# Weight preparation inside the projection's program, and 25 units of row maxima placed in its last six chunks

## The chip, the cores and the metric

One core of one Trainium2 chip runs the whole program. The metric is the device time of one launch in microseconds. Shown are the median of three runs and one profiled execution.

## The reference

For x of 8 batches x 1024 tokens x 256 features, in float32:

```
xn = layernorm(x)
Q, K, V = xn wq^T, xn wk^T, xn wv^T     # 16 heads of 16; RoPE on Q and K
s  = softmax(causal(Q K^T / 4)) V wo^T
g  = silu( (silu(xn wg^T) * (xn wu^T)) wd^T )   # wg, wu, wd: int32 / 127, hidden 768
out = x + s * g
```

The four attention weights are 256 x 256 float32. The three FFN weights are integers from -127 to 127.

## The kernel before

The program has three blocks, one behind the other; at each border all engines meet.

**The preparation block** (lines 216 to 379). SP loads the four attention weights into raw, the first half of batch 0 of x, gate and up integers, the down integers, the second half of x and the sine and cosine table trig (lines 230 to 238). VectorE takes the absolute maximum of all four weights in one instruction (L309), the layer norm's statistics of the first 512 tokens (L168, L175), and builds a power-of-two scale per weight (L314 to L325). TensorE transposes every weight in 128 x 128 pieces through PSUM, 19 banks in all (L378). For the four float weights ScalarE writes the high float16 part (L350) and VectorE the low one (L334). For the integers VectorE casts to float32 (L330), and the two engines take the transposed banks in turn (L301, L355). VectorE normalises the first tokens (L184) after the four weights. GpSimd clears vs, fills ks (L261), and computes the inverse root (L192, L194) and the low part of the tokens (L204). ScalarE writes their high part (L199), and SP issues two DMA transposes (L213), which give xTh and xTl.

**The projection block** (lines 393 to 702) works through 16 chunks of 512 tokens, two per batch. Batches 0 to 6 are a hardware loop, the last batch is written out (`over_batches`). In a chunk TensorE does Q and K (L639, three products of high and low parts), V (L647), the six gate and up products (L662) and the down products of high and low parts (L676). VectorE turns Q and K (L484), multiplies gate by up (L493) and takes low parts; ScalarE takes high parts, SiLU and the copies; GpSimd adds the rotation's terms (L544) and takes low parts (L452, L460). While a chunk runs, the next chunk's tokens are normalised, split and transposed. Results go to HBM. With the last batch SP also loads the stacks of three head groups for the attention of batch 0 (`load_stacks`, L754 to L757; 24 DMAs in one place).

**Units of maxima.** The attention needs each query's largest score before it exponentiates. A group is 4 heads of one batch, 32 groups in all. Its maxima are 18 units: TensorE computes two PSUM banks of scores (L773, causal mask added by L781), and VectorE reduces them (L797, `maximum`). Then `join_max` (L1118) joins the pieces, TensorE transposes the 32 x 128 result (L1340), `negate_max` (L1124) scales and negates it, `split_max` on GpSimd (L1045, L1047) makes two float16 rows, and `load_max` on SP (L986) writes them by 4 DMAs into the query stacks, where they ride along in the score matmul. The projection block holds 17 units of group (0,0) in its last two chunks, at places named after the work they follow (`peek`, PSUM banks 0 and 1):

```
PEEKS = ({"ffn1": 0, "ffn2": 1, "ffn3": 2, "ffn4": 3, "down0": 4, "down2": 5, "down4": 6},
         {"q0": 7, "q1": 8, "k0": 9, "ffn1": 10, "ffn2": 11, "ffn3": 12, "ffn4": 13, "down0": 14, "down2": 15, "down4": 16})
```

**The attention block** begins with `first_maxima`: unit 17 of group (0,0), its join, transpose, negation, split and load, and 7 units of group (0,1). Then come the 32 groups, written out. In a group TensorE follows a hand-written order of 36 turns, 18 E (a score matmul L1316 for ScalarE's exponential L1245) and 18 M (a unit of maxima of a coming group), over three pairs of PSUM banks; a turn waits until the instruction that read its pair three turns before is done (`wait_slot`). Products with V (L1333), output transposes (L1353, L1361) and the output projection (L1369) stand at fixed turns. The first score of a group waits for its maxima rows (mx_ld).

Of the kernel before, what the change touches and what calls it, by code (L numbers as in the profile page):

```python
# [13 lines left out]
P = 128  # L14
# [58 lines left out]
def earlier(step, n):  # L73
    return step[0], step[1] - n
# [14 lines left out]
def project_phase(nc, ps, keep, x, wq, wk, wv, wo, w_gate, w_up, w_down, cs, scratch):  # L89
# [5 lines left out]
    with ctx:  # L95
# [9 lines left out]
        wguT = sb("wguT", [P, 2, KD, HID], F16)  # L105
        wdT = sb("wdT", [P, MH, D], F16)
        trig = sb("trig", [P, 2, 2, S], F32)
        table = sb("table1", [1, 1], F32)
        negh = sb("negh", [P, CT], F32)
# [13 lines left out]
        s_const = sem("s_const")  # L123
        s_ones = sem("s_ones")
        s_one = sem("s_one")
        s_max, s_maxT, s_scale, s_low = sem("s_max"), sem("s_maxT"), sem("s_scale"), sem("s_low")
        s_held = sem("s_held")
        s_unfilled = sem("s_unfilled")
        s_wload = sem("s_wload")
        s_iload = [sem(f"s_iload{i}") for i in range(3)]  # L130
        s_prep = sem("s_prep")
        s_wt = sem("s_wt")
        s_we = [sem(f"s_we{i}") for i in range(2)]
# [82 lines left out]
        with ExitStack() as pre, nc.Block() as block:  # L216
            raw = pre.enter_context(nc.sbuf_tensor("raw", [P, 8, D], F32))
            rawi = pre.enter_context(nc.sbuf_tensor("rawi", [P, 18, D], I32))
            rawf = pre.enter_context(nc.sbuf_tensor("rawf", [P, 18, D], F32))
            wmax = pre.enter_context(nc.sbuf_tensor("wmax", [P, 4], F32))  # L220
            wmaxT = pre.enter_context(nc.sbuf_tensor("wmaxT", [4, 1], F32))
            ones4 = pre.enter_context(nc.sbuf_tensor("ones4", [4, P], F32))
            diag4 = pre.enter_context(nc.sbuf_tensor("diag4", [4, 4], F32))
            wbits = pre.enter_context(nc.sbuf_tensor("wbits", [P, 4], I32))
            wscale = pre.enter_context(nc.sbuf_tensor("wscale", [P, 4], F32))
            SCALE_STEPS = 9

            @block.sync
            def _(sp):
                for i, w in enumerate((wq, wk, wv, wo)):  # L230
                    sp.dma_start(raw[:, 2 * i:2 * i + 2, :], w.rearrange("(m p) d -> p m d", p=P)).then_inc(s_wload, 16)
                sp.dma_start(xs[:, 0], x_v[0, 0]).then_inc(x_ld[0].sem, 16)
                for i, w in enumerate((w_gate, w_up)):
                    sp.dma_start(rawi[:, 6 * i:6 * i + 6, :], w.rearrange("(m p) d -> p m d", p=P)).then_inc(s_iload[i], 16)
                sp.dma_start(rawi[:, 12:18, :].rearrange("p (a m) e -> p a (m e)", a=2),
                             w_down.rearrange("(a p) e -> p a e", p=P)).then_inc(s_iload[2], 16)
                sp.dma_start(xs[:, 1], x_v[0, 1]).then_inc(x_ld[1].sem, 16)
                sp.dma_start(trig[:, :, :, :], cs[:, :, :, :]).then_inc(s_const, 16)
                for s in (t_hi, t_lo):
                    s.start(sp)  # L240
                transpose_tokens(sp, (0, 0))

            @block.gpsimd
            def _(pool):
                for s in (ln_ve, ln_rs, x_lo):
                    s.start(pool)
                ch = Chain(pool, s_prep)
                ch(pool.memset(ident[:, :], 0.0))
                ch(pool.affine_select(out=ident[:, :], in_=ident[:, :], compare_op=ALU.not_equal, fill=1.0,
                                      base=0, pattern=[[-1, P]], channel_multiplier=1))  # L250
                ch(pool.memset(ones4[:, :], 1.0))
                ch(pool.memset(identh[:, :], 0.0))
                ch(pool.affine_select(out=identh[:, :], in_=identh[:, :], compare_op=ALU.not_equal, fill=1.0,
                                      base=0, pattern=[[-1, P]], channel_multiplier=1))
                ch(pool.memset(negh[:, :], -0.5))
                ch(pool.memset(table[:, :], 0.0))
                ch(pool.memset(vs[:, :, :, :], 0.0))
                ch(pool.memset(vs[:, :, :, DK:DK + 1], 1.0))

                for g in range(NG):  # L260
                    pool.memset(keep["ks"][g].rearrange("p j s -> p (j s)").bitcast(F32), MAX_UNITS).then_inc(s_ones, 1)  # L261
                inverse_root(pool, (0, 0))
                low_tokens(pool, (0, 0))


            banks = []
            split = []
            for i in range(4):
                srcs = [raw[:, 2 * i + m, kd * P:(kd + 1) * P] for kd in range(KD) for m in range(2)]
                flat = lambda t: t.rearrange("p k e -> p (k e)")  # L270
                banks.append((srcs, []))
                if i < 2:

                    split.append([([wqkT[:, hl, kd, 2 * i + eo, :].rearrange("p (i h) -> p i h", h=H) for hl in range(2)], kd, eo)
                                  for kd in range(KD) for eo in range(2)])
                else:
# [1231 lines left out]
```

## Time and profile before

| what | us |
|---|---|
| median of 3 runs (1251.95 to 1253.29) | 1253.18 |
| the profiled execution | 1253.75 |
| its span, first to last instruction | 1252.0 |
| TensorE busy | 1196.9 |
| VectorE busy | 1009.0 |
| ScalarE busy | 851.2 |
| GpSimd busy | 601.7 |
| mean granted TensorE clock | 0.985 |

The profile's engines are PE (TensorE), PEld (its weight loads), DVE (VectorE), ACT (ScalarE), POOL (GpSimd) and SPq (the DMA issues of SyncE). A bracket at the end of a timeline row gives how long the engine stood idle before it and who released it. Matmul durations overlap the next matmul, so the distance of two starts says what one costs.

### The profile page before, as it was taken

Reading aid. Unit: us, or ns where it says so; the run is one execution under the profiler, and the core shown is the slowest. Engines: PE = TensorE matmul, PEld = TensorE weight load, DVE = VectorE, ACT = ScalarE, POOL = GpSimd, SP = SyncE. Lnnn points to the kernel's source line nnn. Section 1 sums busy time; section 2 is a strip of 40 time slices with the busy share of each in tenths; the row PEclk is TensorE's granted clock in tenths of the full one; section 3 lists DMA queues with packets and bytes.
Section 4 is the critical chain, followed back from the end, with each engine's and each line's share of the span. In section 5 each row is a group of like instructions: output and inputs, shape, how many; then the busy total and the mean of one; then the engine's idle time right before and its main releaser. Section 6 shows DMA issues by size and latency. Waiting matters only on the chain.

```text
span 1252.0 us, 30431 instructions
## 1 busy us (share of the span) xinstructions
PE 1196.9 (96%) x10743; PEld 558.0 (45%) x10743; DVE 1009.0 (81%) x1229; ACT 851.2 (68%) x1074; POOL 601.7 (48%) x934
## 2 busy tenths in 40 slices
PE   4999999999999799999999999999999999999997
PEld 3556656656654333334433443344334433443333
DVE  5666666666668789899999999999999999999943
ACT  3455465465453367678887888788788878887884
POOL 4665665665663222235444544454445345534554
PEclk9999999999999789999999999999999999999999
DMA  7444544544565311223313323243143233331222
GB/s 243 128 145 165 163 145 161 166 146 157 168 155 153 97 44 44 77 59 106 94 44 111 79 86 95 62 119 95 45 116 103 57 95 82 99 95 44 70 70 85
DMA packets 152228, 133.48 MB, mean 107 GB/s; under 512 B 44720, under 2 KB 137392, under 8 KB 151984
## 3 DMA queue, kind: packets, MB, share of 16 engines
q1 hardware_dynamic: 152112, 131.90, 35.7%
q8 instruction: 77, 1.26, 0.4%
q14 instruction: 39, 0.32, 0.1%
HBM read 72.61 MB, written 50.33 MB: 98 GB/s over the span
## 4 chain that ended last, share of the span: by engine, by line
PE 56%; issue 5%; DVE 2%; ACT 1%; DMA 1%; SPq 1%; POOL 0%; DVEq 0%; ACTq 0%; POOLq 0%
PE ps L1333 21%; PE ps L1316 13%; PE ps L773 11%; PE ps L1369 4%; PE ps L781 3%; PE ps L1353 3%; DVE mxp L797 2%; PE ps L1361 2%; ACT pr L1245 1%; DMA qs<-mp 1%; PE ps L1340 1%; SPq L986 1%; ACT ot L1252 0%; DVE yt L1181 0%; POOL ah L1065 0%
## 5 line engine op out<-in xcount | busy, mean ns | idle before, releaser
L797 DVE TENSOR_REDUCE mxp<-ps 128x2 f32<-128x1024 f32 (+2 forms) x576 | 683.6, 1222 | 64.8 <-PE ps L773 37.0
L1245 ACT ACTIVATE pr<-ps 128x1024 f32<-128x1024 f32 x576 | 570.0, 1033 | 172.1 <-PE ps L1316 164.5
L1333 PE MATMUL ps<-pr,vt 128*32 128x512 f32 (+3 forms) x3072 | 316.5, 500 | 1.4 <-ACT ot L1252 0.9
L1055 POOL TENSOR_SCALAR_AFFINE_SELECT pr<-pr 128x256 f32<-128x256 f32 (+1 forms) x448 | 192.1, 449 | 125.8 <-ACT pr L1245 124.6
L1316 PE MATMUL ps<-qs,ks 50*128 50x512 f16 (+3 forms) x1536 | 227.1, 331 | 14.2 <-DMA qs<-mp 3.5
L773 PE MATMUL ps<-ks,qs 48*128 48x512 f16 (+2 forms) x1792 | 228.0, 308 | 9.8 <-DVE mxp L797 5.0
L1045 POOL TENSOR_SCALAR mp<-mneg 32x128 f16<-32x128 f32 x32 | 9.2, 288 | 319.2 <-issue 305.6
L1316 PEld LDWEIGHTS ps<-qs,ks 50*128 50x128 f16 x1536 | 64.8, 94 | 214.2 <-issue 205.9
L662 PE MATMUL ps<-xTh,wguT 128*128 128x512 f16 x384 | 145.9, 380 | 1.5 <-ACT vs L571 1.2
L662 PE MATMUL ps<-xTl,wguT 128*128 128x512 f16 x384 | 145.8, 380 | 0.0
L773 PEld LDWEIGHTS ps<-ks,qs 48*128 48x128 f16 x1792 | 82.1, 94 | 138.1 <-issue 119.2
L493 DVE SCALAR_TENSOR_TENSOR h<-ps,sg 128x512 f32<-128x512 f32 x96 | 66.0, 688 | 59.3 <-ACT sg L579 44.3
L1333 PEld LDWEIGHTS ps<-pr,vt 128*32 128x32 f32 x3072 | 67.7, 109 | 86.2 <-issue 76.3
L566 ACT ACTIVATE parts<-rr 128x1024 f16<-128x1024 f32 x32 | 33.8, 1057 | 79.1 <-POOL rr L544 79.1
L781 PE MATMUL ps<-future,pick 64*128 64x128 bf16 (+3 forms) x1024 | 86.6, 245 | 0.0
L579 ACT ACTIVATE sg<-ps 128x512 f32<-128x512 f32 x96 | 57.1, 595 | 39.9 <-PE ps L662 30.9
L460 POOL TENSOR_TENSOR hl<-h,hh 128x512 f16<-128x512 f32 x64 | 72.8, 1157 | 21.3 <-ACT hh L585 21.2
L639 PE MATMUL ps<-xTh,wqkT 128*128 128x512 f16 x256 | 80.7, 385 | 2.4 <-DMA xTl<-xl 2.4
L544 POOL TENSOR_TENSOR rr<-rot 128x1024 f32<-128x1024 f32 x32 | 74.8, 2363 | 15.2 <-DVE rot L484 15.2
L484 DVE TENSOR_TENSOR rot<-ps,trig 128x1024 f32<-128x1024 f32 x64 | 75.3, 1219 | 8.4 <-PE ps L639 8.4
L585 ACT ACTIVATE hh<-h 128x512 f16<-128x512 f32 x96 | 58.3, 624 | 4.7 <-DVE h L493 4.0
L662 PEld LDWEIGHTS ps<-xTh,wguT 128*128 128x128 f16 x384 | 37.4, 97 | 47.6 <-DVE h L493 3.3
(107 smaller groups left out, 1315.6 us busy)
## 6 DMA issues: line engine op xcount, KB each, us to landing
v_d<-vs SPq DMA_DIRECT2D x16, 1024.0 KB, 4.9
vt<-v_d SPq DMA_DIRECT2D x32, 512.0 KB, 4.1
xs<-in_L_attn_x SPq DMA_DIRECT2D x16, 512.0 KB, 4.2
q_parts_d<-parts SPq DMA_DIRECT2D x16, 512.0 KB, 2.9
k_parts_d<-parts SPq DMA_DIRECT2D x16, 512.0 KB, 2.9
gate_d<-gs SPq DMA_DIRECT2D x16, 512.0 KB, 3.2
qs<-q_parts_d SPq DMA_DIRECT2D x64, 128.0 KB, 3.0
ks<-k_parts_d SPq DMA_DIRECT2D x64, 128.0 KB, 3.1
```

The costliest lines, as they stand in the source:

```text
L460: eng.tensor_tensor(hl[:, m], h32[:, m % NH], hh[:, m], ALU.subtract).then_inc((lo_pool if m < LOW_POOL else lo_dve).sem, 1)
L484: ins = dve.tensor_tensor(tq[i][:, t], ps[:, (Q0, K0)[i]:(Q0, K0)[i] + 2, :], trig[:, t, :, c * CH:(c + 1) * CH], ALU.mult)
L544: pool.tensor_tensor(rr[i][:, :, :], tq[i][:, :, 0, :], tq[i][:, :, 1, :], ALU.add).then_inc(rot_add.sem, 1)
L639: ins = pe.matmul(ps[:, (Q0, K0)[i] + eo, :], wqkT[:, wp, kd, 2 * i + eo, :], xx[:, c, :, kd, :], start=n == 0, stop=n == len(terms) - 1)
L662: ins = pe.matmul(ps[:, FFN[m] + gu, :], wguT[:, gu, kd, m * P:(m + 1) * P], xx[:, c, :, kd, :], start=n == 0, stop=n == 2 * KD - 1)
L773: ins = pe.matmul(ps[:, slot + t, n * w:(n + 1) * w], qs[r, j, qb * P:(qb + 1) * P], ks[r, j, lo:lo + w], start=n == 0, stop=not any(maske ...
L781: ins = pe.matmul(o, pick[r, half ^ t, :], future[r, half ^ t, 0:len(pieces), half * TILE:P], start=False, stop=half == 1, skip_group_chec ...
L797: dve.tensor_reduce(dst, ps[:, slot:slot + 2, :].rearrange("p t (n s) -> p (t n) s", s=w), axis=AX.X, op=ALU.max).then_inc(keep["max_dve"] ...
L1055: pool.affine_select(out=blk, in_=blk, compare_op=ALU.is_ge, fill=0.0, base=0, pattern=[[0, 2], [0, len(hs)], [1, P]], channel_multiplier= ...
L1245: act.activation(probs(step, s).rearrange("p (t j) s -> p t j s", t=2)[:, :, hs[0]:hs[-1] + 1, 0:w], ps[:, slot:slot + 2, 0:w * len(hs)].r ...
L1316: ins = pe.matmul(ps[:, slot + t, o:o + w], ks[g][r, j, kb * P:(kb + 1) * P], qs[g][r, j, lo:lo + w], start=o == 0, stop=True, skip_group_ ...
L1333: ins = pe.matmul(ps[VW * j:VW * (j + 1), O0, lo - c * CH:CH], vt[g % 2][:, kb, j, :], probs(step, s)[:, j, at:at + w], start=first, stop= ...
```

## The change

The preparation block goes. Its work moves into the projection block, ahead of and into the first chunk:

- SP loads x first, then the weights, each with a semaphore of its own. The table trig is loaded in two halves by token half, each in two DMAs, between the other loads.
- VectorE takes one maximum per weight: three before the normalisation of the first tokens, one after. The float weights are still transposed by TensorE and split by ScalarE and VectorE; query and key parts come before the first chunk, V's in its beginning, and wo's low part after the low part of Q.
- The integers are cast by ScalarE to float16 and transposed by three DMA transposes on SP, with no work of TensorE or VectorE. wguT and wdT have another layout for it.
- GpSimd clears vs and builds identh in the first chunk, and the constants of pick and future at its end; before, they stood ahead of the first chunk.
- Before the loop now stands batch 0 written out, then a loop over batches 1 to 4, then batches 5 to 7 written out.
- The 17 units in the last two chunks become 25 in the last six: all 18 of group (0,0) in five chunks, and in the last one 7 of group (0,1). The join's transpose stands at place q0 of the last chunk, then negation, split and load of the maxima in the projection's block. `first_maxima` goes from the attention block, whose first TensorE instruction is now the first score.
- SP loads one head group's stacks per chunk, in three chunks.

```diff
-        with ExitStack() as pre, nc.Block() as block:
...
             def over_batches(eng, chunk):
 
-                with eng.Fori(0, B - 1) as b:
+                for c in range(HALVES):
+                    chunk((0, c), True)
+                with eng.Fori(1, B - WRITTEN_OUT) as b:
                     for c in range(HALVES):
                         chunk((b, c), True)
-                for c in range(HALVES):
-                    chunk((B - 1, c), c + 1 < HALVES)
+                for b in range(B - WRITTEN_OUT, B):
+                    for c in range(HALVES):
+                        chunk((b, c), (b, c) != (B - 1, HALVES - 1))
 
             @block.sync
             def _(sp):
...
+                sp.dma_start(xs[:, 0], x_v[0, 0]).then_inc(x_ld[0].sem, 16)
+                for i, w in enumerate((wq, wk, wv, wo)):
+                    sp.dma_start(raw[:, 2 * i:2 * i + 2, :], w.rearrange("(m p) d -> p m d", p=P)).then_inc(s_wload[i], 16)
+                sp.dma_start(xs[:, 1], x_v[0, 1]).then_inc(x_ld[1].sem, 16)
+                for i, w in enumerate((w_gate, w_up)):
+                    sp.dma_start(rawi[:, MH * i:MH * (i + 1), :], w.rearrange("(m p) d -> p m d", p=P)).then_inc(s_iload[i], 16)
...
+                def transpose_ints(i):
+                    sp.wait_ge(s_cast, i + 1)
+                    dst = wguT[:, i].rearrange("p m k t -> p (m k) t") if i < 2 else wdT.rearrange("p k m t -> p (k m) t")
+                    sp.dma_start_transpose(dst[:, :, :], rawh[:, MH * i:MH * (i + 1), :].rearrange("p m d -> p (m d)")).then_inc(s_ints[i], 16)
+
+                transpose_tokens(sp, (0, 0))
+                load_trig(0)
+                sp.dma_start(rawi[:, 2 * MH:3 * MH, :].rearrange("p (a m) e -> p a (m e)", a=2),
+                             w_down.rearrange("(a p) e -> p a e", p=P)).then_inc(s_iload[2], 16)
+                transpose_ints(0)
+                transpose_ints(1)
+                load_trig(1)
+                transpose_ints(2)
...
                 over_batches(sp, chunk)
+                load_max(sp, keep, (0, 0))
...
+                stats(dve, (0, 0))
+                for i in range(3):
+                    weight_max(i)
+                normalise(dve, (0, 0))
+                weight_max(3)
...
+                stats(dve, (0, 1))
+                weight_low(0)
+                weight_low(1)
...
+                high_tokens(act, (0, 0))
+                act.wait_ge(s_wt, 4)
+                act.wait_ge(s_scale, SCALED)
+                weight_high(0)
+                weight_high(1)
+                weight_high(2)
+                cast_ints(0)
+                cast_ints(1)
...
                 def peek(step, place):
-                    if isinstance(step[0], int) and place in PEEKS[step[1]]:
...
+                    if joined(step) and place == "q0":
+                        transpose_max(pe, ps, keep, (0, 0), T0)
+                    if peeked(step, place):
+                        ms, u = peeked(step, place)
+                        if ms == (0, 1) and u == 0:
+                            pe.wait_ge(keep["mx_neg"].sem, keep["mx_neg"].after((0, 0)))
...
+WRITTEN_OUT = 3
+SHIFT = 7
+PLACES = (((3, 0), ("down0", "down2")), ((3, 1), ("ffn1", "ffn3", "down0", "down2")), ((2, 0), ("ffn1", "ffn3", "down0", "down2")),
+          ((2, 1), ("ffn1", "ffn3", "down0", "down2")), ((1, 0), ("ffn1", "ffn3", "down0", "down2")),
+          ((1, 1), ("q1", "k0", "ffn1", "ffn2", "ffn3", "ffn4", "down0")))
+PEEKED = [((0, 0), u) for u in range(18)] + [((0, 1), u) for u in range(SHIFT)]
...
-                for n, (ms, u) in enumerate(first_maxima):
-                    if n == 0:
-                        pe.wait_ge(max_dve.sem, max_dve.after((0, 0), PEEKED))
-                    if n >= SLOTS:
-                        pe.wait_ge(max_dve.sem, max_dve.after(first_maxima[n - SLOTS][0], first_maxima[n - SLOTS][1] + 1))
-                    queries_by_keys(pe, ps, keep, s_held, ms, u, slot_of(n - len(first_maxima)))
-                    if (ms, u) == ((0, 0), NM - 1):
-                        transpose_max((0, 0))
```

## Rows read from the trace of the kernel before

**Rows 1.** The page's part 1: busy time, share, instructions.

```profile
PE 1196.9 (96%) x10743; PEld 558.0 (45%) x10743; DVE 1009.0 (81%) x1229; ACT 851.2 (68%) x1074; POOL 601.7 (48%) x934
```

**Rows 2.** Windows by stage: length; busy us of each engine; clock; DMA share, GB/s.

```profile
0.00:28.31 28.31, 10.70 (x56) 9.32 (x56) 16.65 (x45) 9.17 (x21) 11.71 (x22) 0.94 0.73 250
...
56.68:337.48 280.80, 280.80 (x1730) 168.88 (x1728) 184.92 (x301) 150.29 (x228) 175.38 (x120) 1.00 0.49 157
...
359.65:387.02 27.37, 26.87 (x176) 14.71 (x174) 20.38 (x23) 12.68 (x21) 14.41 (x9) 1.00 0.89 202
387.02:417.24 30.22, 28.79 (x192) 15.07 (x190) 24.68 (x23) 10.81 (x18) 11.37 (x7) 1.00 0.24 88
...
429.64:458.64 29.00, 25.98 (x207) 8.56 (x208) 23.43 (x24) 17.90 (x19) 6.03 (x15) 0.73 0.08 17
458.64:484.33 25.69, 23.17 (x242) 8.64 (x243) 23.77 (x25) 19.12 (x21) 6.97 (x17) 1.00 0.20 56
```

**Rows 3.** Timeline of the start: start us, us, engine, line, instruction, tiles.

```profile
3.09 1.80 POOL L257 MEMSET vs<- 128x2048 f32 x1
4.50 2.53 SPq L235 DMA_DIRECT2D rawi<-in_L_ffn_w_down  x1
5.22 3.62 POOL L261 MEMSET ks<- 128x1024 f32 x4
6.98 2.29 DVE L309 TENSOR_REDUCE wmax<-raw 128x4 f32<-128x2048 f32 x1 [6.98 <-DMA raw<-in_L_attn_wo]
...
11.70 1.03 POOL L194 TENSOR_TENSOR rstd<-ve,negh 128x4 f32<-128x4 f32 x1
...
13.69 2.17 ACT L350 ACTIVATE wqkT<-ps,wscale 128x128 f16<-128x128 f32 x8 [10.42 <-DVE oscale L325]
14.87 1.12 DVE L334 SCALAR_TENSOR_TENSOR wqkT<-ps,wscale,wqkT 128x128 f16<-128x128 f32 x4 [0.21 <-ACT wqkT L350]
...
20.00 1.37 DVE L184 TENSOR_SCALAR xn<-xs,mv,rstd 128x256 f32<-128x256 f32 x4
...
28.31 0.39 PE L639 MATMUL ps<-xTh,wqkT 128*128 128x512 f16 x1 [2.42 <-DMA xTl<-xl]
...
37.80 0.38 PE L662 MATMUL ps<-xTh,wguT 128*128 128x512 f16 x1
```

**Rows 4.** Windows in which the granted clock is low, columns as in rows 2.

```profile
29.00:32.00 3.00, 3.00 (x8) 1.06 (x7) 1.24 (x7) 0.00 (x0) 2.33 (x6) 0.50 0.50 159
...
508.00:510.00 2.00, 0.31 (x5) 0.03 (x1) 1.77 (x2) 1.02 (x1) 1.18 (x3) 1.00 0.24 84
510.00:512.00 2.00, 2.00 (x12) 0.43 (x12) 1.00 (x1) 1.02 (x1) 0.19 (x2) 0.53 0.80 211
```

**Rows 5.** DMA landing: the tile xTh, and the issues of trig by line.

```profile
DMA to landing us min/median/max: 2.8/3.5/5.8
...
trig<-in_trig SPq DMA_DIRECT2D x1, 2048.0 KB, 13.5
```

**Rows 6.** Timeline of TensorE around two units in the last chunk.

```profile
388.11 0.38 PE L639 MATMUL ps<-xTh,wqkT 128*128 128x512 f16 x1
...
388.83 0.39 PE L639 MATMUL ps<-xTh,wqkT 128*128 128x512 f16 x1
...
403.10 0.39 PE L773 MATMUL ps<-ks,qs 48*128 48x512 f16 x2 [0.97 <-DVE mxp L797]
```

**Rows 7.** Timeline from the last down matmuls to the first score.

```profile
415.03 1.05 PE L676 MATMUL ps<-wdT,hl 128*128 128x256 f16 x8
...
417.35 0.37 SPq L432 DMA_DIRECT2D gate_d<-gs  x1
...
420.03 0.40 PE L773 MATMUL ps<-ks,qs 48*128 48x128 f16 x8 [2.80 <-issue]
...
423.79 10.46 DVE L797 TENSOR_REDUCE mxp<-ps 128x2 f32<-128x1024 f32 x9 [0.26 <-PE ps L773]
...
429.64 0.61 PE L1316 MATMUL ps<-qs,ks 50*128 50x512 f16 x2 [0.48 <-DVE mxp L797]
```

More of the change, by code:

```diff
@@ L398, in nxt, with peeked, joined, is_first @@
                 return step[0], step[1] + 1
+            def peeked(step, place):
+                return PEEKS.get((B - step[0], step[1]), {}).get(place) if isinstance(step[0], int) else None
+            def joined(step):
+                return isinstance(step[0], int) and step == (B - 1, HALVES - 1)
+            def is_first(step):
+                return isinstance(step[0], int) and step == (0, 0)
             def over_batches(eng, chunk):
-                with eng.Fori(0, B - 1) as b:
+                for c in range(HALVES):
+                    chunk((0, c), True)
+                with eng.Fori(1, B - WRITTEN_OUT) as b:
@@ L498, in chunk @@
                     if more:
-                        stats(dve, nxt(step))
+                        if not is_first(step):
+                            stats(dve, nxt(step))
                         normalise(dve, nxt(step))
-                    peek(step, "q0")
+                    if is_first(step):
+                        weight_low(2)
+                    if joined(step):
+                        negate_max(dve, ps, keep, (0, 0), T0)
                     peek(step, "q1")
@@ L554, in chunk @@
                         low(pool, step, m)
+                    if is_first(step):
+                        constants()
                 over_batches(pool, chunk)
@@ L588, in chunk @@
                 def chunk(step, more):
-                    if step[1] == 0:
+                    if step[1] == 0 and not is_first(step):
                         act.activation(table[:, :], table[:, :], ACT.Silu).then_inc(s_held, 1)
@@ L676, in down @@
                             ins = pe.matmul(ps[:, V0 + a // 2, (a % 2) * D:(a % 2 + 1) * D], part[:, m, a * P:(a + 1) * P],
-                                            wdT[:, m, :], start=part is hh and m == 0 and a % 2 == 0,
+                                            wdT[:, :, m, :], start=part is hh and m == 0 and a % 2 == 0,
                                             stop=part is hl and m == MH - 1, skip_group_check=True)
@@ L695, in _ @@
                 over_batches(pe, chunk)
-PEEKS = ({"ffn1": 0, "ffn2": 1, "ffn3": 2, "ffn4": 3, "down0": 4, "down2": 5, "down4": 6},
-         {"q0": 7, "q1": 8, "k0": 9, "ffn1": 10, "ffn2": 11, "ffn3": 12, "ffn4": 13, "down0": 14, "down2": 15, "down4": 16})
-PEEKED = sum(len(p) for p in PEEKS)
+WRITTEN_OUT = 3
[4 more added lines that the diff above has]
+PEEKED = [((0, 0), u) for u in range(18)] + [((0, 1), u) for u in range(SHIFT)]
+PEEKS = {}
+for chunk, places in PLACES:
+    PEEKS[chunk] = {place: PEEKED[sum(len(p) for p in PEEKS.values()) + n] for n, place in enumerate(places)}
+assert sum(len(p) for p in PEEKS.values()) == len(PEEKED)
 def key_steps():
```

411 lines of the change are left out of this document (179 added, 232 removed).

## The prediction

> **What bounds the kernel now.** I read the page's first part, then the windows by stage, then the timeline at the two places that the change touches. TensorE is busy for 96% of the span [rows 1]. The windows show where it is not, and that is what the change can win [rows 2]. From 0 to 28.31 us the weights are prepared and TensorE works for 10.70 us. In the 280.8 us that hold twelve of the sixteen chunks TensorE is busy for all 280.80, which makes 23.40 us for a chunk: no chunk there waits for VectorE, ScalarE or a transfer, so whatever else a chunk contains is free, and only matmuls cost. The last two chunks take 27.37 and 30.22 us, because 17 units of maxima stand in them. Between the end of the last of them, 417.24, and the first score at 429.64 lie 12.40 us. The first group of the attention takes 29.00 us, the next 25.69, at a granted clock of 0.73 against 1.00. The change works on all four places and leaves the other 31 groups alone.
>
> **Part 1, the start (saves 10.2 us).** Now the chain to the first projection matmul is: four weights land, their maximum ends at 9.27, then scales, splits and casts on VectorE hold back the normalisation of x until 20.00, and from there x hi and lo, two DMA transposes and the wait for xTl bring TensorE to 28.31 [rows 3]. The stretch from 20.00 to 28.31 (8.31 us) stays: same instructions, same queue. What moves is the 20.00. In the changed order VectorE does the statistics, three of the four weight maxima (2.29 us for four, 0.57 each) and then normalises. It waits for the later of two things. GpSimd: its memsets of ks take 3.62 us and began at 5.22, behind those of vs (from 3.09) and of identh, which now come later; I let them begin at 2.4 and end at 6.0, and with ve (0.2) and rstd (1.03), some 1.3 us with the gaps, it is 7.4. Weights: wo landed at 6.98 with 1 MB in front of it and itself; wv now lands behind 1.25 MB, since 512 KB of x go first. I put it at 7.5 to 8, so its maximum ends at 8.5. So 8.5 plus 8.31 gives the first query matmul at **16.8**. The other condition, the split query weights: the fourth maximum ends at 8.5 + 1.37 + 0.57 = 10.5, the transposed maximum and the scale chain took from 9.27 to ScalarE's first split at 13.69, with 1.9 us of statistics between, so 2.5 more gives 13.0, then 1.1 us on ScalarE (2.17 for eight), the statistics of the second half on VectorE until about 15.1, and 1.12 us of low parts: 16.2 [rows 3]. That is just in time. Saved 11.5 us. Bounds for this start: 15.7 (GpSimd alone decides, 7.4 + 8.31) and 19 (the weights and, behind them, the gate and up integers hold the tokens' transposes up by 2 us).
>
> In the first chunk, which is now also the place of the weights, I charge 1.3 us. The clock is one part: with TensorE nearly idle before it, the first chunk ran 3 us at a granted 0.50 (1.2 GHz) [rows 4], which cost 1.5 us; now it works less before, so I take half as much again, 0.8 us, bounds 0 and 1.7. Of the rest: wv's and wo's low parts (0.7 us each on VectorE), ScalarE's three casts of 1536 columns and GpSimd's memsets lie beside matmuls, and cost nothing as long as the chunk's slack covers them; VectorE is busy 15.4 of 23.4 us in a chunk and GpSimd 14.6 (184.92 and 175.38 in twelve), so GpSimd also has room for the constants of the mask, which now stand at that chunk's end ahead of the next normalisation. I charge 0.5 for the low part ahead of the first hidden product. The gate and up weights must be there 9.5 us after the first query matmul (they were at 28.31 and 37.80), gate at 26.3 and up 0.9 us later, at 27.2. SP reaches their transposes after the 2.53 us issue of w_down at about 18.6; a transpose of 8 blocks lands in 2.8 to 3.5 us as a rule [rows 5], so 12 blocks in 4.2 to 5.3, the second issued 1.9 us later: up at 25.8. It is hidden by 1.4 us. The Trainium skill, DMA: Bandwidth & Descriptors, section on latency and other measured facts, gives 261 GB/s for a DMA transpose, by which 384 KB would take 1.5 us; the rows here show a slower one, and the sum goes by them. The sine tables now come in two pieces: the whole took 13.5 us in a crowd [rows 5], the first half is needed at 20. The fifteen evacuations of integer banks vanish with the block.
>
> **Part 2, the units in the chunks (costs 4.4 us).** One unit adds 0.5 us to TensorE: the query matmul before it starts at 388.11, the next at 388.83, where 0.22 (23.40 us over the chunk's columns) is normal [rows 6]. I use that for all. The last two chunks until the last down matmul at 416.08 took 56.43 us for 46.8: 9.6 us for 16 units, of which 0.97 is one wait for VectorE, which has a maximum of 1.2 us for each [rows 6, 7]. Now 25 units: 12.6 us with the masks, the matmul that transposes the joined maxima 0.4, and waits. With four units in a chunk VectorE has 15.4 + 4.9 of 25.4 us to do, so no wait; in the last chunk there are seven instead of ten, and none at its end. I take 1.0 us, bounds 0 and 3. The join waits for unit 17's maximum: 1.23 + 0.25 us on VectorE against 0.9 us of down matmuls and 1.3 of the first query matmuls, so it is covered by 0.5 us. The negation has the next six query matmuls for itself. GpSimd's split waits for the negation with rotated(0) behind it, which comes later anyway. Sum 14.0 against 9.6. The stack loads (8 DMAs per group) are spread over three chunks instead of one; the last chunks' transposes waited for them, and TensorE did not.
>
> **Part 3, the seam (saves 9.6 us).** From the last down matmul at 416.08 to the first score at 429.64 are 13.56 us [rows 7]. What stays: ScalarE's gate and its store until 417.72, and from there 2.31 us until TensorE's first instruction of the new block at 420.03. What goes: unit 17, join, transpose, negation, split, the load of the maxima, and seven maxima of the next group, which on VectorE run from 423.79 without a pause (nine in 10.46 us) and release the first score when the fifth is done, because of its PSUM slot. So 3.95 us remain. The exp table's load and the v load start in this gap; v lands about 3.5 us behind the first score and is wanted after about 6.
>
> **Part 4, the first group (saves 1.0 us).** It loses the two maxima still outstanding at 429.64, which held its first three turns, 1.5 us; ScalarE's table may give 0.5 back. It stays a group at half clock: TensorE is idle some 4 us at the seam, and before, the gap of 2.80 us with a thin stretch behind it ended in the 0.73 of this group, and 508 to 510, with 0.31 us busy, in 0.53 [rows 2, 4, 7]. Bounds: 0, and 3.3 if it takes 25.7 like its neighbours.
>
> **Sum.** 10.2 - 4.4 + 9.6 + 1.0 = 16.4 us. The profiled execution took 1253.75 us (its span 1252.0 and 1.75 around it), so 1237.35; the median of the runs is 0.57 lower, which gives 1236.8, say **1237**.
>
> **Rivals.** (a) The clock holds at the seam, so the first group takes 25.7 us: 2.3 us more, 1234.5. For it: the gap now is not followed by a thin stretch of seven maxima but by scores at once. Against it: the two falls named. The Trainium skill, TensorE: Matmul & The Clock Gate, Part 1, says an idle stretch leaves the engine at 1.2 GHz until it has been busy again; by that this rival would be dead and the sum stays. Chance 0.2. (b) The first chunk stalls: tokens behind the integer loads, then the integer transposes late. The longest landing of an xTh transpose was 5.8 us [rows 5]; 12 blocks at that rate take 8.7, so up's weights arrive at 29.2, 2.0 late, and with the first matmul at 19 (2.2) and a clock that stays down longer (0.9) it is 5 us: 1242. Chance 0.15. (c) Slower: the same integer transposes, if a transpose of 12 blocks next to table and weight loads takes over 12.5 us. Gate's and up's run one behind the other from 18.6, so up's land past 43.6 instead of by 27.2, the first chunk's FFN matmuls are over 16.4 us late, and everything after moves by it; at 15 us each it is 21.4 late, 1258. For it speaks only trig's 13.5 us in a crowd, against it sixteen transposes with at most 5.8. Chance 0.03. (d) The seam keeps part of its time, since the first score is held by another late thing at the seam (exp table, v load, the registers that ScalarE loads): then up to 4 us come back, 1241. Chance 0.07. The forecast itself gets 0.55.
>
> **Range and chances.** The forecast's own terms move by -1.1 and +2.2 (start), -1 and +2 (waits in the last chunk), and by later falls of the clock like that at 510 [rows 4]: some three microseconds at half speed cost 1.5, and whether one more or one fewer comes is open. With (a), (b) and (d) inside: 1230 to 1244. A measurement here tells 0.2%, 2.5 us, from nothing. Only (c) and unknown mishaps reach there: faster 0.95, same 0.02, slower 0.03.
>
> **What would show it.** Right: first query matmul near 16.8, chunks of 23.40 between, about 25.4 with four units, first score 4 us behind the last down matmul, first group about 28 us with a clock near 0.7. Wrong: a DMA that releases the first gate matmul, waits on VectorE in the chunks with four units, a first score released by ScalarE or a load, or groups after the first that are not 25.0 us.

## The result, and the profile after

The kernel after takes **1244.61 us** in the median of 4 runs (1242.65 to 1245.75); the kernel before, beside it, 1253.24 (1251.95 to 1254.45). The ratio is 0.9934, interval 0.9915 to 0.9953: 0.7% faster, clear of the noise. That is 8.6 us, where 16.4 were forecast; 1244.61 lies 0.6 us above the range. The profiled execution took 1243.78 us, its span is 1242.0.

Part 1 of the page answers to [rows 1]:

```profile
PE 1188.8 (96%) x10707; PEld 548.3 (44%) x10707; DVE 1002.9 (81%) x1221; ACT 842.2 (68%) x1062; POOL 602.6 (49%) x935
```

TensorE lost 8.1 us of work and the span 10.0, so the shares look as before. Only cuts by stage tell more. I cut both traces at the same events: the first query matmul, the stores of gate_d that end the chunks, the first score, the first scores of the second and the fourth group, the end. The columns of changes sum to the span's difference; spans are taken to 0.1 us. The right column is the same pair of programs, profiled once more in the last experiments.

| stretch | before | after | change | once more |
|---|---|---|---|---|
| to the first query matmul | 28.31 | 18.89 | -9.42 | -10.59 |
| first chunk, to its store | 28.37 | 27.46 | -0.91 | -1.07 |
| second chunk | 23.44 | 24.93 | +1.49 | +1.49 |
| next eight chunks | 187.18 | 187.29 | +0.11 | +0.11 |
| last six chunks | 150.05 | 162.41 | **+12.36** | +12.35 |
| last store to first score | 12.29 | 4.75 | -7.54 | -7.53 |
| first group | 29.00 | 26.18 | -2.82 | -0.46 |
| second and third group | 51.36 | 49.61 | -1.75 | -1.41 |
| the rest | 742.00 | 740.48 | -1.52 | +1.41 |
| span | 1252.0 | 1242.0 | -10.0 | -5.7 |

The windows of the last six chunks (one of six is left out) and of the second chunk (length; busy us of each engine; clock; DMA share, GB/s) answer to [rows 2]:

```profile
258.57:282.84 24.27, 24.27 (x153) 14.11 (x152) 16.35 (x22) 11.65 (x18) 13.40 (x8) 1.00 0.71 185
282.84:310.25 27.41, 25.97 (x166) 14.24 (x165) 19.53 (x30) 11.68 (x19) 14.61 (x10) 1.00 0.59 164
310.25:337.39 27.14, 25.69 (x154) 13.90 (x153) 19.51 (x30) 11.68 (x19) 14.61 (x10) 1.00 0.55 166
...
364.88:392.69 27.81, 26.37 (x178) 14.31 (x176) 19.13 (x28) 11.69 (x19) 14.59 (x10) 1.00 0.37 114
392.69:420.98 28.29, 26.33 (x172) 14.22 (x170) 21.27 (x21) 10.70 (x17) 12.07 (x9) 1.00 0.26 94
46.35:71.28 24.93, 23.77 (x146) 13.85 (x145) 15.09 (x25) 11.67 (x19) 16.23 (x14) 1.00 0.52 149
```

Four units in a chunk cost 27.1 to 27.8 us where 25.4 were forecast, though VectorE is busy 19.1 to 19.5 us there, less than the 20.3 that I had added up, and TensorE stands idle for 1.4 us. No engine lacks time: an order of work is in the way. The timeline of VectorE, GpSimd and TensorE's waits at such a border shows it:

```profile
280.92 1.23 DVE L815 TENSOR_REDUCE mxp<-ps 128x2 f32<-128x1024 f32 x1 [1.21 <-PE ps L799]
...
282.06 1.40 DVE L170 BATCH_NORM_STATS2 st<-xs 128x6 f32<-128x256 f32 x4
...
284.26 0.19 POOL L194 TENSOR_SCALAR ve<-mv 128x4 f32<-128x4 f32 x1 [7.38 <-issue]
284.54 1.02 POOL L196 TENSOR_TENSOR rstd<-ve,negh 128x4 f32<-128x4 f32 x1
285.70 1.38 DVE L186 TENSOR_SCALAR xn<-xs,mv,rstd 128x256 f32<-128x256 f32 x4 [1.62 <-POOL rstd L196]
286.99 4.61 DVE L423 TENSOR_TENSOR rot<-ps,trig 128x1024 f32<-128x1024 f32 x4
...
291.66 0.39 PE L671 MATMUL ps<-xTh,wguT 128*128 128x512 f16 x1 [0.28 <-DVE rot L423]
...
294.92 0.39 PE L671 MATMUL ps<-xTh,wguT 128*128 128x512 f16 x1 [1.04 <-ACT vs L557]
```

VectorE takes the maximum of the unit at down2 (280.92) before the statistics of the coming tokens (282.06), because that is where it stands in its program. Behind the statistics come GpSimd's variance and rstd, the normalisation, and only then the rotation of Q and K (286.99 to 291.6), whose PSUM banks the gate and up products need: TensorE waits at 291.66, and at 294.92 for ScalarE's copy of V, which is late behind the same chain. Both waits stand at each of the four borders behind units among the down matmuls, 5.3 us in all.

The start, from the normalisation to the first query matmul, answers to [rows 3]:

```profile
10.01 0.40 DVE L186 TENSOR_SCALAR xn<-xs,mv,rstd 128x256 f32<-128x256 f32 x1
...
11.71 2.12 POOL L206 TENSOR_TENSOR xl<-xn,xh 128x1024 f16<-128x1024 f32 x1 [2.83 <-ACT xh L201]
11.78 2.06 DVE L395 TENSOR_TENSOR diag<-ident,wmaxT 4x4 f32<-4x4 f32 x1
...
15.45 2.17 ACT L532 ACTIVATE wqkT<-ps,wscale 128x128 f16<-128x128 f32 x8 [3.89 <-DVE wscale L400]
15.59 1.40 DVE L170 BATCH_NORM_STATS2 st<-xs 128x6 f32<-128x256 f32 x4
...
17.54 1.61 DVE L382 SCALAR_TENSOR_TENSOR wqkT<-ps,wscale,wqkT 128x128 f16<-128x128 f32 x6
...
18.89 0.58 PE L645 MATMUL ps<-xTh,wqkT 128*128 128x512 f16 x1 [4.41 <-DVE wqkT L382]
```

A product of 4 x 4 elements took 2.06 us on VectorE, and ended when GpSimd's low part of the tokens did (11.71 + 2.12). The low parts of the query weights (the first four of L382), the later of my two conditions here, ended at 18.6 where I had 16.2: 0.5 us are the fourth maximum, which ended at 11.0 and not at 10.5, and 1.9 us the long product. The tokens were not late: xTl had landed at 17.0, against 16.8 in the forecast.

The seam answers to [rows 7]:

```profile
418.08 1.91 PE L685 MATMUL ps<-wdT,hl 128*128 128x256 f16 x16
419.87 1.09 ACT L599 ACTIVATE gs<-ps 128x512 f32<-128x512 f32 x2 [3.36 <-PE ps L685]
420.98 0.37 SPq L331 DMA_DIRECT2D gate_d<-gs  x1
421.39 2.74 SPq L858 DMA_DIRECT2D qs<-mp  x4
...
425.73 0.61 PE L1327 MATMUL ps<-qs,ks 50*128 50x512 f16 x2 [5.74 <-DMA qs<-mp]
```

The last down matmul ends at 419.99 and the first score starts 5.74 us behind it, not 3.95: the load of the joined maxima stands in SP's order behind the last gate store, whose data comes from ScalarE at 420.96.

### The profile page after: what moved, and what is told of

Read it like the earlier page. It is cut to its first block, busy times and chain, and to the rows that moved or that the text cites. A ratio compares the mean times of both kernels' runs of the same rounds, so it can differ in the third digit from the quotient of the medians.

```text
span 1242.0 us, 29795 instructions
## 1 busy us (share of the span) xinstructions
PE 1188.8 (96%) x10707; PEld 548.3 (44%) x10707; DVE 1002.9 (81%) x1221; ACT 842.2 (68%) x1062; POOL 602.6 (49%) x935
## 4 chain that ended last, share of the span: by engine, by line
PE 58%; issue 3%; ACT 2%; DVE 1%; DMA 1%; POOL 0%; SPq 0%; ACTq 0%; DVEq 0%; POOLq 0%
PE ps L1344 22%; PE ps L1327 13%; PE ps L791 11%; PE ps L1374 4%; PE ps L799 3%; PE ps L1358 3%; ACT pr L1256 2%; PE ps L1366 2%; PE ps L830 1%; DMA qs<-mp 1%; DVE mxp L815 0%; SPq L858 0%; ACT ot L1263 0%; DVE yt L1192 0%; POOL ah L1096 0%
## 5 line engine op out<-in xcount | busy, mean ns | idle before, releaser
L791 PE MATMUL ps<-ks,qs 48*128 48x512 f16 (+2 forms) x1792 | 225.1, 304 | 5.4 <-DVE mxp L815 2.1
```

Source lines behind the costliest of these rows:

```text
L791: ins = pe.matmul(ps[:, slot + t, n * w:(n + 1) * w], qs[r, j, qb * P:(qb + 1) * P], ks[r, j, lo:lo + w], start=n == 0, stop=not any(maske ...
```

## The experiments

All kernels but the last two are variants of the kernel after, 1244.61 us. The kernel before stood beside the first four at 1253.01 us, beside the next four at 1254.05 and beside the last two at 1254.25, so differences of medians are good to about 1 us; where a trace cuts out the stretch that an edit changes, that is the firmer number. The expectations number the theories as they came; theory 1 is VectorE's order in the chunks.

### VectorE's statistics ahead of the units

```diff
-                        if not is_first(step):
-                            stats(dve, nxt(step))
                         normalise(dve, nxt(step))
...
+                    if not isinstance(step[0], int) or step[0] < B - 1:
+                        stats(dve, nxt(nxt(step)))
                     for n in range(CT + 1):
                         peek(step, f"down{n}")
```

> The 25 units stay at their places; only on VectorE the statistics of the chunk after the next move from behind the maxima of down0 and down2 (the start of the next chunk) to ahead of them. Theory 1 (order): the maximum of down2 holds back statistics, inverse root, normalisation and so the rotation of Q, which releases the first gate matmuls late; chunks with four units took 27.1 to 27.8 us in the changed kernel for 25.4 worked out. Then they fall to about 25.5, the wait for rot goes, and the kernel gains some 7 to 8 us: about 1237. Rival 2 (load): VectorE has too much to do in a chunk with four units, whatever the order; then the chunks stay at 27 and the time at 1244. Rival 3: a unit costs TensorE more than the 0.5 us that I took; same outcome as rival 2, but with no idle time of TensorE.

Measured: 1241.72 us (1239.93 to 1242.29), ratio 0.9902 [0.9886, 0.9919], so 2.9 us less than the kernel after. The last six chunks take 25.65, 26.93, 26.75, 26.92, 26.05, 28.29 us, together 160.59: they give only 1.8 us of the 2.9, and the trace shows no other stretch that the edit shortens. TensorE's waits and VectorE's instructions at the same border:

```profile
281.10 0.39 PE L791 MATMUL ps<-ks,qs 48*128 48x512 f16 x2 [1.31 <-DVE mxp L815]
```

```profile
277.82 1.40 DVE L170 BATCH_NORM_STATS2 st<-xs 128x6 f32<-128x256 f32 x4
...
279.75 1.20 DVE L815 TENSOR_REDUCE mxp<-ps 128x2 f32<-128x1024 f32 x1
```

The wait for the rotation is gone, and another stands in its place: the unit at down2 needs the banks of the unit at down0, whose maximum now waits behind the statistics. The order matters, but two units among the down matmuls leave no good one: whichever goes first, the other holds TensorE.

### Units among the gate and up products instead

```diff
-PLACES = (((3, 0), ("down0", "down2")), ((3, 1), ("ffn1", "ffn3", "down0", "down2")), ...
+PLACES = (((3, 0), ("ffn2", "ffn3")), ((3, 1), ("ffn1", "ffn2", "ffn3", "ffn4")), ...
```

The three chunks behind them likewise; the last chunk keeps its places.

> Same number of units in every chunk, same order of VectorE's other work, but no unit at down0 or down2: two units at ffn2, ffn3 and four at ffn1 to ffn4 in place of ffn1, ffn3, down0, down2. Theory 1: nothing stands ahead of the next chunk's statistics, so the chunks fall to 25.4 to 26 us and the kernel to 1236 to 1239. Rival 2 (load) and rival 3 (cost on TensorE): no change, 1244. A third outcome: the units at neighbouring ffn places wait for each other on the one pair of banks, 0.3 to 0.5 us each; then about 1240.

Measured: **1237.83 us** (1235.89 to 1239.93), ratio 0.9871 [0.9853, 0.9889]: 6.8 us less than the kernel after. The chunks take 24.51, 25.68, 25.40, 25.75, 26.08 and 28.29 us. A chunk with four units now costs what I had forecast, with the same units and the same maxima on VectorE; only their places are others. The last six chunks together take 155.71 us, 6.7 less than in the kernel after. In the two windows that I compared, 282.85 to 333.93 us here, each is 1.74 us shorter than its counterpart in the kernel after: 1.2 of it is idle time (the two waits of 1.3 are gone, and one of 0.2 for the neighbouring unit's banks is new), and TensorE counts 0.5 us less as busy, which I did not follow further. This is the larger part of what was missing.

### One operand fewer for the 4 x 4 product

```diff
-                ch(dve.tensor_tensor(diag4[:, :], ident[0:4, 0:4], wmaxT[:, :].to_broadcast([4, 4]), ALU.mult))
+                ch(dve.tensor_scalar(diag4[:, :], ident[0:4, 0:4], wmaxT[:, 0:1], None, ALU.mult))
```

> The diagonal of the weight scales is made by a tensor-scalar instruction with one tensor from SBUF in place of a tensor-tensor one with two. In the changed kernel this 4 x 4 instruction took 2.06 us and ended with GpSimd's low part of the tokens (11.71 to 13.83), where before it took 0.15. Theory 4 (shared access): VectorE with two tensors from SBUF waits for GpSimd's running instruction; then it takes about 0.2 us now, the first query matmul comes 1.9 us earlier, at 17.0, and the kernel gains 1 to 2 us (1242.5 to 1243.5; a tokens' transpose or a longer slow clock may take a part). Rival: the instruction is long because it waits for GpSimd's identity or for a semaphore; then nothing moves.

Measured: 1244.52 us (1244.08 to 1246.75), no change. The rows of GpSimd and VectorE:

```profile
11.65 2.12 POOL L206 TENSOR_TENSOR xl<-xn,xh 128x1024 f16<-128x1024 f32 x1 [2.84 <-ACT xh L201]
11.72 2.06 DVE L395 TENSOR_SCALAR diag<-ident,wmaxT 4x4 f32<-4x4 f32 x1
```

With one tensor from SBUF it is held just as long, so the second tensor is not what makes it wait.

### The load of the maxima ahead of the last store

```diff
+                    if joined(step):
+                        load_max(sp, keep, (0, 0))
...
                 over_batches(sp, chunk)
-                load_max(sp, keep, (0, 0))
```

The two new lines stand in SP's program of the last chunk, ahead of its gate store.

> SP issues the four DMAs of group (0,0)'s maxima before the last chunk's gate store instead of behind it. Theory 5: in the changed kernel these issues (421.39, 2.74 us) stood behind the gate store at 420.98, held the end of the block, and the first score waited for their landing, 5.74 us behind the last down matmul. Then the first score comes 3.9 us behind the last down matmul, 1.8 us earlier, and the time is about 1242.5. Rival: something else at the border (the exp table's load, the first instructions of the block) holds the first score at about 5 us; then 0.5 us or less.

Measured: 1242.30 us (1240.51 to 1242.61), ratio 0.9913 [0.9896, 0.9929]: 2.3 us less. The issues of SP:

```profile
408.72 3.18 SPq L859 DMA_DIRECT2D qs<-mp  x3
419.59 0.39 SPq L333 DMA_DIRECT2D gate_d<-gs  x1
```

and TensorE's first score:

```profile
421.45 0.61 PE L1328 MATMUL ps<-qs,ks 50*128 50x512 f16 x2 [2.85 <-PEq L254]
```

The load starts 10.9 us before the store, and the first score starts 2.85 us behind the last down matmul (418.60), released by nothing but the change of block. That is 2.9 us less at the seam, where 1.8 were expected; the rival (something else holds the first score at 5 us) is out.

### The 4 x 4 product on ScalarE

```diff
-                ch(dve.tensor_tensor(diag4[:, :], ident[0:4, 0:4], wmaxT[:, :].to_broadcast([4, 4]), ALU.mult))
+                act.activation(diag4[:, :], ident[0:4, 0:4], ACT.Copy, scale=wmaxT[:, 0:1])
```

> Edit: the 4x4 diagonal of the weights' maxima is made by ScalarE, by a copy with a scale, so VectorE does nothing between the transposed xh and the low parts. Theory 3 (while GpSimd's tensor_tensor of the tokens' low part runs, 2.12 us, VectorE does not get through any instruction of its own that it starts in that time): the 4x4 copy is done by ScalarE in about 0.2 us, but the next small instruction of VectorE's scale chain becomes the long one and ends with GpSimd's at about 13.8; the scale is ready about 1 us sooner than 15.36, the first query matmul comes at about 18.0 instead of 18.9, and the time is 1 us lower, 1243.6. Rival (the diagonal itself was slow, on whichever engine): ScalarE takes about 2 us for it and nothing moves. Rival (one-column operations with integer bits are not held): the whole chain comes 1.9 us sooner, first query matmul at 17.0, 1242.7.

```profile
11.78 2.12 POOL L206 TENSOR_TENSOR xl<-xn,xh 128x1024 f16<-128x1024 f32 x1 [2.83 <-ACT xh L201]
11.86 0.30 ACT L540 ACTIVATE diag<-ident,wmaxT 4x4 f32<-4x4 f32 x1 [0.22 <-DVE wmaxT L393]
...
12.89 0.16 DVE L396 COPY wscale<-ps 128x4 f32<-128x4 f32 x1 [1.07 <-PE ps L620]
13.09 0.84 DVE L397 TENSOR_SCALAR wbits<-wscale 128x4 int32<-128x4 int32 x1
```

ScalarE takes 0.30 us. The next VectorE instruction that works from SBUF to SBUF is now the long one, 0.84 us, and ends at 13.93, with GpSimd's at 13.90; the copy from PSUM ahead of it takes 0.16 us although GpSimd is at work. So theory 3 holds with one correction: what is held is not every instruction of VectorE, but those that only touch SBUF. The first query matmul comes at 17.87, one microsecond sooner, as expected. The time, 1244.83 us (1242.97 to 1245.75), does not show it: one microsecond is less than executions of one program differ by here, as the last experiments show.

### The mask's constants in two parts

```diff
                 def more_constants():
...
+                    if isinstance(step[0], int) and step == (0, 1):
+                        more_constants()
```

> Edit: GpSimd makes the constants of the mask in two parts, behind its work of chunk (0,0) and of chunk (0,1), instead of all 5.6 us in one piece ahead of the next normalisation. Theory 4 (these constants are what makes the second chunk 24.93 us instead of 23.40, because GpSimd's variances, the normalised tokens and the first rotation all come late behind them): the second chunk takes about 23.6 us, the third stays at 23.4 to 23.6, and the time is 1.3 us lower, 1243.3. Rival (the second chunk is late from the first one's ScalarE and VectorE work, or the half of the constants that moves on holds the third chunk as it held the second): the two together take the same 48.4 us.

Measured: 1243.70 us (1243.14 to 1244.22), ratio 0.9922 [0.9894, 0.9951], 0.9 less. In its trace the second chunk takes 23.46 us instead of 24.93, and the third 23.50 as before: the 1.47 us were the constants, which in the kernel after keep GpSimd until 46.85 and the variance of the next tokens until 47.06. In two parts they cost nothing.

### Three edits together

> Edit: three edits together, the units of the five chunks behind four FFN blocks instead of behind down matmuls, the load of the joined maxima ahead of the last gate store, and the constants in two parts. If the three causes (VectorE's order in the chunks, SP's order at the seam, GpSimd's constants) are separate places of the chain, their gains add: 6.8 from the first, 2.3 from the second, 1.3 from the third, so 1244.6 - 10.4 = 1234.2 us, with chunks of 25.4 to 26.1 us where four units stand, and the first score 2.9 us behind the last down matmul. Rival (they overlap, or later groups give some back): 1236 or more.

Measured: **1235.09 us** (1234.05 to 1235.21), ratio 0.9853 [0.9824, 0.9881]. 9.5 us below the kernel after, where the three alone gave 6.8, 2.3 and 0.9: they add. The trace shows it stretch by stretch: the last six chunks take 155.65 us (155.71 with the first edit alone), the first score stands 2.86 us behind the last down matmul (2.85), and the second chunk takes 23.47 us (23.46). Of the windows of its last six chunks, the first, the second and the last:

```profile
255.77:280.29 24.52, 24.43 (x153) 14.12 (x152) 17.24 (x27) 11.64 (x18) 14.53 (x10) 1.00 0.73 183
280.29:305.94 25.65, 25.44 (x166) 14.52 (x165) 19.71 (x29) 11.77 (x19) 14.61 (x11) 1.00 0.64 175
...
383.12:411.42 28.30, 26.34 (x172) 14.19 (x170) 21.30 (x21) 10.69 (x17) 12.05 (x9) 1.00 0.27 94
```

All six together take 155.65 us, 5.6 over the kernel before's 150.05. The forecast for the units was 4.4.

### And the tokens' low part on VectorE

```diff
+                low_tokens(dve, (0, 0))
...
-                stats(dve, (0, 1))
                 weight_low(0)
+                stats(dve, (0, 1))
...
-                low_tokens(pool, (0, 0))
```

> Edit: as the run before, and the low part of the first chunk's tokens is made by VectorE behind the diagonal instead of by GpSimd, with the low part of the first query weights ahead of the statistics of the second chunk. Theory 3: with nothing on GpSimd beside it, the diagonal takes about 0.1 us instead of 2.06, VectorE's low part of 512 columns takes 0.6 to 1.2 us, the first query matmul comes at about 17.0 instead of 18.9, and the time is 1.9 us below the run before: 1232.3. Rival (TensorE starts earlier but is then held by the weights of the first chunk, or runs at half clock for longer): the first query matmul comes at 17.0, and the time is the same as in the run before.

```profile
11.78 0.15 DVE L396 TENSOR_TENSOR diag<-ident,wmaxT 4x4 f32<-4x4 f32 x1
11.96 1.23 DVE L206 TENSOR_TENSOR xl<-xn,xh 128x1024 f16<-128x1024 f32 x1
...
16.60 0.58 PE L651 MATMUL ps<-xTh,wqkT 128*128 128x512 f16 x1 [4.24 <-DMA xTl<-xl]
...
30.61 0.39 PE L677 MATMUL ps<-xTh,wguT 128*128 128x512 f16 x1 [0.76 <-ACT vs L563]
...
33.21 0.39 PE L677 MATMUL ps<-xTh,wguT 128*128 128x512 f16 x1 [0.70 <-DVE h L434]
```

With GpSimd idle the same instruction takes 0.15 us, started at the same 11.78. The first query matmul comes at 16.60, now released by the tokens. But the time is 1236.15 us (1235.38 to 1237.90), not less than 1235.09: the rival holds, in its first form, since the half clock was not longer here but shorter (3.4 us behind the first query matmul, 5.1 in the run before). The first chunk's store stands at 44.81 against 45.01 in the run before, though TensorE began 1.24 us earlier. TensorE now waits 1.46 us in the gate and up products, for ScalarE's copy of V and VectorE's hidden product; both engines have the weights' work besides their own there. Behind the start the first chunk itself is the next limit, and little is left to win by an earlier first matmul alone.

### Both kernels once more

No edit: the two programs, profiled a second time, in one execution each.

> The kernel before, unchanged, profiled a second time. Theory 5 (the two waits of 1.32 and 1.69 us for the transfer of the split maxima at the turns of the second and third group belong to the kernel before, because its first group ends later against its own loads): they are there again, with the second and third group at 25.7 us. Rival (how long such a small transfer takes to land differs from one execution to the next): one or both are gone, those groups take 24.8 us, and 2.9 of the 9.97 us between the two profiled executions are no effect of the change.

1253.19 us. The chunks are those of [rows 2] to 0.05 us, and the first group takes 28.88. The fourth group begins at 509.58:

```profile
484.48 0.39 PE L1316 MATMUL ps<-qs,ks 50*128 50x512 f16 x2 [1.55 <-DVE mxp L797]
509.58 0.39 PE L1316 MATMUL ps<-qs,ks 50*128 50x512 f16 x2 [1.13 <-DMA qs<-mp]
```

The two waits are there again, one with another releaser: the second and third group take 51.02 us, against 49.61 in both traces of the kernel after and 49.61 to 49.80 in its variants. So 1.4 to 1.75 us come from the change. What in it removes them was not tried.

> The kernel after, unchanged, profiled a second time. The chunks are expected within 0.1 us of the first trace (24.93, 23.4, 24.3, 27.4, 27.1, 27.5, 27.8, 28.3), since VectorE's order is fixed. Two things may differ: which of the diagonal on VectorE and the low part on GpSimd starts first (at 11.78 and 11.71 in the first trace; where VectorE is first, the diagonal takes 0.15 us, the long instruction is the next one on SBUF alone, and the first query matmul comes at 17.9 instead of 18.9), and how long the first chunk stays at half clock (2.5 to 5.7 us in the traces so far, 1.6 us of time). Rival (both are fixed by the program): 18.89 and 46.35 again within 0.1.

1247.60 us, 3.8 above the first profiled execution. The fifteen chunks behind the first agree to 0.02 us. The start does not:

```profile
11.62 0.15 DVE L395 TENSOR_TENSOR diag<-ident,wmaxT 4x4 f32<-4x4 f32 x1
...
12.51 1.29 DVE L398 TENSOR_SCALAR wbits<-wscale 128x4 int32<-128x4 int32 x1
```

GpSimd's low part began at 11.66 here. VectorE was first by 0.04 us, the product took 0.15 us, and the next instruction on SBUF alone was held to the same end, 13.80. The first query matmul came at 17.74, 1.15 us sooner than in the first trace by this chance alone. The first group's windows in the two traces of this program (first the one shown above, then this):

```profile
425.73:451.91 26.18, 23.21 (x206) 7.85 (x207) 21.27 (x22) 18.40 (x21) 6.05 (x15) 0.83 0.33 71
```

```profile
424.44:452.86 28.42, 25.68 (x206) 8.52 (x207) 21.37 (x22) 18.50 (x21) 6.03 (x15) 0.73 0.31 66
```

Same work, 2.24 us apart by the granted clock, 0.83 or 0.73: it stood at 0.50 for 10.2 us around the seam in the first trace, and for 17.1 in the second. Over ten traces of the kernel after and its variants this group takes 26.2 to 28.9 us. The 1.8 us by which it beat my forecast in the first trace are therefore no surplus of the change, and neither are the 1.5 of "the rest", which the second pair gives back; in the first trace of the kernel before they contain the fall of the clock at 510 us [rows 4], which stands in no other trace.

## Why the prediction was wrong

**Right: the direction and the places.** Twelve old chunks and eight new ones take 23.4 us, so work on other engines is free there. The integer transposes were hidden: those of gate and up landed 5.1 and 4.3 us after their issue, up's at 26.05, as forecast, and the first gate matmul started at 29.58, so rival (c) is out. Of rival (b) the longer half clock came, and a first query matmul at 18.89, but held by the query weights and not by the tokens. The first group runs in part at half clock: 28.42 us in one trace where 28.0 was forecast, 26.18 in the other, never 25.7 in ten traces, so rival (a), that the clock holds, is out, though in the first trace the time came near it.

**The step that failed most: "With four units in a chunk VectorE has 15.4 + 4.9 of 25.4 us to do, so no wait".** The sum of busy time was nearly right (20.3 us, 19.1 to 19.7 measured) and the conclusion wrong. VectorE takes its instructions in program order in these traces, and the units at down0 and down2 stand ahead of the statistics on which the next chunk's rotation hangs; in the kernel before no chunk but the last two had such units. I never wrote down what is queued behind a unit's maximum. It cost 12.36 us where 4.4 stood. With the same units at other places it costs 5.6: 6.7 of the 8.0 missing come with these places (6.8 in the medians, 1244.61 to 1237.83). The other 1.3 were not followed.

**The start, -10.2 forecast, -8.8 measured** (-9.42 - 0.91 + 1.49; -10.17 once more). The first query matmul came at 18.89 and 17.74 instead of 16.8. I let the scale chain cost what it cost before, where GpSimd had only two instructions of 128 x 4 beside it. Now GpSimd's low part of the tokens lies beside it and holds it for 1.9 us in one trace and 1.1 in the other. With the tokens' low part on VectorE and the low part of the query weights ahead of the statistics, the first query matmul comes at 16.60.

The first and second chunk together were forecast 1.3 us dearer, and are 0.6 (0.4) dearer, but in other terms. The clock, forecast at 0.8, cost about 1.0: TensorE stayed at half clock until 5.9 and 5.5 us behind the first query matmul, against 3.8 and 3.6 in the two traces of the kernel before. The mask's constants of GpSimd, which I costed at nothing because GpSimd is busy 14.6 of 23.4 us, cost 1.5 us in the second chunk, since they stand ahead of the variance that the next normalisation waits for. It is the same mistake as above on another engine. And I missed that they had already cost this in the kernel before, in its first chunk, where they stood ahead of the same variance: VectorE had the statistics ready at 30.4, and GpSimd reached the variance at 32.6. TensorE then waited here:

```profile
39.94 0.39 PE L662 MATMUL ps<-xTh,wguT 128*128 128x512 f16 x1 [0.25 <-DVE rot L484]
43.04 0.39 PE L662 MATMUL ps<-xTh,wguT 128*128 128x512 f16 x1 [1.20 <-ACT vs L571]
```

These are the two waits of the four borders above, 1.45 us. That the constants make them is read from the trace here; the run with the constants in two parts shows it for the second chunk. In the kernel after the first chunk has no such wait, which more than pays for its longer half clock, and the second chunk has the cost instead. So the trace before held a sample of the mechanism that the forecast lacked.

**The seam, -9.6 forecast, -7.5 measured.** (From the last down matmul, as the prediction cuts it, it is 13.57 - 5.74 = 7.8, and the units cost 0.3 more.) I wrote that the load of the maxima goes from the seam, and took its DMAs as early ones. In SP's order they follow the last gate store, and the first score waits for their landing. Moved ahead of it, the first score stands 2.85 us behind the last down matmul, 1.1 sooner than the 3.95 that I had. This was rival (d) in kind, a late thing at the seam, but not one of the three that I named for it.

**Not in the forecast:** the second and third group, 1.4 to 1.75 us faster. Against the first trace, 8.0 (units), 1.4 (start) and 2.1 (seam) are missing, 1.8 (first group), 1.75 and 1.5 came in addition: 16.4 - 11.5 + 5.1 = 10.0, the span's difference. The range was too narrow because waits were bounded with up to 3 us for the last chunk, and with nothing for the four chunks ahead of it.

## What to carry to other kernels

An engine with room in a stage is no proof that an added instruction there is free. Ask for each insertion what stands behind it in that engine's program order, and whose chain starts there; if the next stage's critical chain does, put the insertion behind the start of that chain, or at a place in the stage where the queue behind it leads nowhere soon. Do the same for every queue, the DMA queue too: a small load that stands behind a store waits for the store's data.

## What the runs showed of the hardware

A small VectorE instruction with its operands in SBUF can be held for as long as a GpSimd instruction runs: 4 x 4 elements took 2.06 us beside GpSimd's 2.12 us (a tensor pair of 128 x 1024), and 0.15 us with GpSimd idle. One SBUF tensor or two made no difference, a copy from PSUM in the same stretch took 0.16 us, and the one that starts first is not held: a lead of 0.04 us decided where the loss fell. Not every GpSimd instruction holds VectorE: in the kernel before, the scale chain's first instruction on SBUF alone (L319, at 12.49) started while GpSimd computed rstd (11.70 to 12.73) and took 0.17 us, as it does with GpSimd idle. What makes the difference was not tried. The Trainium skill, GPSIMD Engine Reference, section Key points, says that GpSimd shares its SBUF interfaces with VectorE, with contention for instructions of VectorE "in a 2-port perf mode or with two SBUF inputs". The trace agrees for the product with two inputs, 2.06 against 0.15 us; whether the two forms with one input ran in such a mode no run here shows.

TensorE's clock came up late after the start in each of these traces. The first query matmuls stand 0.43 us apart, later ones 0.22: that is the level of 1.2 GHz, then 2.4. Before them TensorE had been busy for 4.61 of 18.89 us in the kernel after. It lasted until 2.9 to 5.9 us behind the first query matmul. Two traces of one program:

```profile
23.53 1.06 PE L645 MATMUL ps<-xTh,wqkT 128*128 128x512 f16 x2
24.39 0.58 PE L645 MATMUL ps<-xTl,wqkT 128*128 128x512 f16 x1
```

```profile
22.39 1.06 PE L645 MATMUL ps<-xTh,wqkT 128*128 128x512 f16 x2
23.24 0.43 PE L645 MATMUL ps<-xTl,wqkT 128*128 128x512 f16 x1
```

In the first of them the column of the granted clock shows 1.00 from 19 to 24 us, although the matmuls stand 0.43 us apart; in the second it shows 0.50 from 17 to 23. Where the two disagree, the distance of the starts is what costs time.
